# Self-attention of a perceiver block: scores in sixteen 32x32 tiles, and the residual added on TensorE

## The reference, cut to what matters

```
x = x + attn(layernorm(x))
q = (x @ w_q)  -> 16 heads of 8;   k, v = (x @ w_k), (x @ w_v) -> 4 heads of 8, each used by 4 query heads
q, k = rope(q), rope(k)
out = softmax(q k^T / sqrt(8)) v;  out = out @ w_o
```

## Time and profile before

| | |
|---|---|
| time, median of 3 runs | 803.13 us (801.89 to 804.63) |
| the profiled execution | 805.83 us, span 803.8 us |
| mean granted TensorE clock | 0.931 |
| busy: PE, DVE, ACT, POOL | 697.8, 623.8, 510.0, 395.5 us |
| self-attention pipeline | about 502 to 635 us of the span |

### The profile page before, as it was taken

The page is one execution under the profiler, slowest core; times in us unless marked ns, Lnnn a source line. Parts: engine busy times, 40 slices in busy tenths (PEclk is TensorE's granted clock), DMA queues, the critical chain, the costliest instruction groups (busy, mean ns, idle before and its releaser), DMA issues.

```text
span 803.8 us, 27728 instructions
## 1 busy us (share of the span) xinstructions
PE 697.8 (87%) x9162; PEld 563.4 (70%) x9162; DVE 623.8 (78%) x1471; ACT 510.0 (63%) x1629; POOL 395.5 (49%) x409
## 2 busy tenths in 40 slices
PE   4735999999999999999999765899999689999485
PEld 2423776777777777777777644788888578889485
DVE  6415988999999999999999668489888756759621
ACT  2633876777777777777778524688888434545152
POOL 4730664544654455455463168477777310007275
PEclk9976999999999999999999969799999759999698
DMA  7596444444444444444340030000000000006980
GB/s 164 102 208 143 84 79 86 97 86 96 86 97 85 98 85 97 84 98 83 81 84 6 3 105 1 2 3 4 0 0 3 1 1 1 1 1 197 283 264 27
DMA packets 195179, 60.76 MB, mean 76 GB/s; under 512 B 147556, under 2 KB 193512, under 8 KB 195122
## 3 DMA queue, kind: packets, MB, share of 16 engines
q1 hardware_dynamic: 192000, 55.65, 31.5%
q0 software_dynamic: 1824, 3.96, 1.4%
q10 hardware_dynamic: 1298, 0.40, 0.2%
HBM read 51.58 MB, written 8.83 MB: 75 GB/s over the span
## 4 chain that ended last, share of the span: by engine, by line
PE 49%; SPq 16%; DVE 10%; issue 9%; ACT 7%; POOL 4%; ACTq 1%; DMA 1%; DVEq 0%; POOLq 0%
PE energy L487 22%; PE bank L487 15%; PE bank L490 13%; SPq L518 8%; ACT PR L650 6%; DVE X L1778 3%; DVE STAT L1512 2%; SPq L524 2%; POOL SX L947 1%; SPq L541 1%; SPq L566 1%; POOL TQ L939 1%; SPq L577 1%; SPq L568 1%; ACTq L650 1%
## 5 line engine op out<-in xcount | busy, mean ns | idle before, releaser
L650 ACT ACTIVATE PR<-energy,STAT 128x256 f32<-128x256 f32 x512 | 234.4, 482 | 113.2 <-DVE STAT L1512 113.2
L1512 DVE TENSOR_REDUCE STAT<-energy 128x512 f32 (+1 forms) x256 | 164.2, 684 | 26.4 <-PE energy L487 26.4
L490 PE MATMUL bank<-ident,PR 128*128 128x128 f32 x1024 | 152.9, 283 | 27.8 <-DVE PT L1529 23.0
L1529 DVE COPY PT<-bank 128x512 f32<-128x512 f32 x256 | 161.8, 670 | 1.4 <-PE bank L490 1.4
L490 PEld LDWEIGHTS bank<-ident,PR 128*128 128x128 f32 x1024 | 110.1, 142 | 58.6 <-issue 46.1
L845 POOL TENSOR_TENSOR QB<-QT,headmask 128x512 f32<-128x512 f32 x32 | 33.3, 1039 | 190.4 <-DMA MK<-in_mask_BxSxS_ik 120.0
L650 ACT ACTIVATION_READ_ACCUMULATOR PR<-energy,STAT (+1 forms) x512 | 110.2, 215 | 0.0
L852 POOL TENSOR_SCALAR MZ<-MK 128x512 bf16<-128x512 int32 x64 | 94.2, 1488 | 5.3 <-DMA MK<-in_mask_BxSxS_ik 5.3
L487 PEld LDWEIGHTS bank<-wv_s,CT 128*128 128x128 f32 x512 | 67.8, 194 | 31.7 <-issue 31.7
L487 PE MATMUL bank<-PT,VT 128*32 128x128 f32 x2048 | 69.5, 276 | 0.0
L487 PE MATMUL bank<-wv_s,CT 128*128 128x128 f32 x512 | 68.5, 277 | 0.3 <-DVE OC L1521 0.2
(11 more groups left out here) (270 smaller groups left out, 1361.6 us busy)
## 6 DMA issues: line engine op xcount, KB each, us to landing
CX<-in_ctx SPq DMA_DIRECT2D x512, 32.0 KB, 2.3
MK<-in_mask_BxSxS_ik SPq DMA_DIRECT2D x128, 128.0 KB
rows_in<-fill SPq DMA_DIRECT2D x1, 3483.0 KB, 19.6
X<-in_x SPq DMA_DIRECT2D x4, 512.0 KB, 7.7
VLT<-v_last SPq DMA_DIRECT2D x4, 512.0 KB, 9.0
QT<-in_L_ffn_W SPq DMA_DIRECT2D x16, 128.0 KB
OT<-in_L_ffn_W SPq DMA_DIRECT2D x16, 128.0 KB
PAY<-rows_in SPq DMA_DIRECT2D x2, 903.0 KB, 9.2
```

The costliest lines, as they stand in the source:

```text
L490: return nc.tensor.transpose(o, i, ident[0:n, 0:n])
L650: nc.scalar.activation(PR[:, b, g, :], EB[:, g, e * KEYS:(e + 1) * KEYS], ACT.Exp, bias=STAT[:, bass.ds(t, 1), b, 1, g:g + 1].rearrange("p ...
L1512: V.tensor_reduce(STAT[:, bass.ds(t, 1), b:b + 2, 1, g:g + 1].rearrange("p a b g -> p (a b g)"), EB[:, g, :].rearrange("p (e k) -> p e k", ...
L1529: V.tensor_copy(PT[:, k % 2, e, 2 * half:2 * half + 2, :].rearrange("p g k -> p (g k)"), psum[1 if e else 7]).then_inc(ev_t, 1)
```

## The change

- Queries are ordered by group inside each 32 partitions (the weights `wqk` are laid out so), so that the 32 channels of partition block h hold one query head of each of the four key heads. The keys are now the ones spread and masked (`spread_keys`, on GpSimd, in place of spread_queries); own_keys and the clearing of KB are gone.
- scores becomes sixteen matmuls: for each sequence b and each partition block h, 32 channels x 32 queries by 128 keys, written to partitions 32b and bank h of the four energy banks. The output is the same number of scores, in another order; shift_scores and weigh_values read it so.
- The four energy banks are one buffer, and the projection has bank 1 alone: scores(t) waits for the subtraction of tile t-1, project(t) for the rotary of tile t-1.
- project_out adds ident x X[t] into the same accumulation, and ACT `evac_tokens` (in the place of own_keys) copies the sum into X; DVE's residual is gone.
- The PE list becomes await_scores(s-3), project_out(s-6), scores(s-3), project(s-1), ...: the waits of scores stay first, scores itself follows project_out.

```diff
@@ scalar
+            def evac_tokens(t, j):
+                act.wait_ge(a_wo, t + 1)
+                nc.scalar.activation(X[:, bass.ds(t, 1), :].rearrange("p a c -> p (a c)"), psum[7][:, P:2 * P],
+                                     ACT.Copy).then_inc(a_x2, 1)
+
-            def own_keys(t, j):
-
-                act.wait_ge(a_qk, t + 1)
-                wait_reuse(act, a_s, t - 3)
-                for g in range(NG):
-                    rows = slice(g * 32, g * 32 + 32)
-                    last = nc.scalar.activation(KB[rows, j, :, g, :],
-                                                QKR[rows, j, 1, :].rearrange("p (b k) -> p b k", b=BT), ACT.Copy)
-                last.then_inc(a_kb, 1)
-
-            pipeline(act, [(5, evac_probs), (2, own_keys), (0, evac_xv), (1, evac_last_values), (3, exp_scores), (5, evac_o),
+            pipeline(act, [(5, evac_probs), (6, evac_tokens), (0, evac_xv), (1, evac_last_values), (3, exp_scores), (5, evac_o),
                            (-1, centre)], NT, 4, 6)
@@ gpsimd
-            nc.gpsimd.memset(KB[:, :, :, :, :], 0.0).then_inc(zero_ok, 1)
-            def spread_queries(t, j):
+            def spread_keys(t, j):
 
                 pool.wait_ge(a_qk, t + 1)
                 nc.gpsimd.tensor_tensor(
-                    QD[:, j, :, :, :],
-                    QKR[:, j, 0, :].rearrange("p (b a q) -> p b a q", b=BT, a=1).broadcast_to([P, BT, 4, SQ]),
-                    headmask[:, :].rearrange("p (a h c) -> p a h c", a=1, c=1).broadcast_to([P, BT, 4, SQ]),
-                    ALU.mult).then_inc(a_qd, 1)
+                    KB[:, j, :, :, :],
+                    QKR[:, j, 1, :].rearrange("p (b a q) -> p b a q", b=BT, a=1).broadcast_to([P, BT, NG, SQ]),
+                    headmask[:, :].rearrange("p (a h c) -> p a h c", a=1, c=1).broadcast_to([P, BT, NG, SQ]),
+                    ALU.mult).then_inc(a_kb, 1)
@@ tensor
             def project(t, j):
                 pe.wait_ge(a_xt, t + 1)
-                wait_reuse(pe, a_tq, 2 * t - 2)
+                wait_reuse(pe, a_tq, 2 * t)
                 for w in range(4):
-                    last = mm(psum[2 + j % 2][:, w * P:(w + 1) * P], wqk[:, w, :], xt[:, j, :])
+                    last = mm(psum[1][:, w * P:(w + 1) * P], wqk[:, w, :], xt[:, j, :])
                 last.then_inc(a_p, 1)
 
+            def await_scores(t, j):
+
+                pe.wait_ge(a_qk, t + 1)
+                pe.wait_ge(a_kb, t + 1)
+                wait_reuse(pe, a_sx, t)
+
             def scores(t, j):
 
-                pe.wait_ge(a_kb, t + 1)
-                pe.wait_ge(a_qd, t + 1)
-                wait_reuse(pe, a_sx, t - 1)
                 for b in range(BT):
-                    last = mm(psum[4 + j % 2][:, b * P:(b + 1) * P],
-                              QD[:, j, b, :, :].rearrange("p h q -> p (h q)"),
-                              KB[:, j, b, :, :].rearrange("p h q -> p (h q)"))
+                    for h in range(4):
+                        rows = slice(32 * h, 32 * h + 32)
+                        last = mm(EB[32 * b:32 * b + 32, h, 0:P],
+                                  QKR[rows, j, 0, b * SQ:(b + 1) * SQ],
+                                  KB[rows, j, b, :, :].rearrange("p g k -> p (g k)"))
                 last.then_inc(a_s, 1)
 
             def project_out(t, j):
                 pe.wait_ge(a_so, t + 1)
-                mm(psum[7][:, P:2 * P], SO[:, j, :], sw_o[:, :]).then_inc(a_wo, 1)
-
-            pipeline(pe, [(3, scores), (6, project_out), (1, project), (0, turn_x), (5, weigh_values),
+                mm(psum[7][:, P:2 * P], SO[:, j, :], sw_o[:, :], stop=False)
+                mm(psum[7][:, P:2 * P], ident[:, :], X[:, bass.ds(t, 1), :].rearrange("p a c -> p (a c)"), start=False)\
+                    .then_inc(a_wo, 1)
+
+            pipeline(pe, [(3, await_scores), (6, project_out), (3, scores), (1, project), (0, turn_x), (5, weigh_values),
                           (1, self_values), (4, turn_probs)], NT, 4, 6)
@@ vector
-            def residual(t, j):
-                dve.wait_ge(a_wo, t + 1)
-                xi = X[:, bass.ds(t, 1), :].rearrange("p a c -> p (a c)")
-                V.tensor_tensor(xi, xi, psum[7][:, P:2 * P], ALU.add).then_inc(a_x2, 1)
-
-            pipeline(dve, [(4, sum_probs), (4, invert_sums), (6, residual), (3, shift_scores), (6, statistics),
+            pipeline(dve, [(4, sum_probs), (4, invert_sums), (3, shift_scores), (6, statistics),
                            (1, rotary)], NT, 4, 6)
```

More of the change, by code:

```diff
@@ L379, in perceiver_block @@
         a_kb = sem("a_kb")
-        a_qd = sem("a_qd")
         a_s = sem("a_s")
@@ L749, in evac_o @@
                 nc.scalar.activation(SO[:, j, :], psum[7][:, 0:P], ACT.Copy).then_inc(a_so, 1)
-            def own_keys(t, j):
-                act.wait_ge(a_qk, t + 1)
-                wait_reuse(act, a_s, t - 3)
-                for g in range(NG):
-                    rows = slice(g * 32, g * 32 + 32)
-                    last = nc.scalar.activation(KB[rows, j, :, g, :],
-                                                QKR[rows, j, 1, :].rearrange("p (b k) -> p b k", b=BT), ACT.Copy)
-                last.then_inc(a_kb, 1)
-            act.wait_ge(zero_ok, 1)
             act.wait_ge(n1_shift, 1)
             centre(0, 0)
-            pipeline(act, [(5, evac_probs), (2, own_keys), (0, evac_xv), (1, evac_last_values), (3, exp_scores), (5, evac_o),
+            pipeline(act, [(5, evac_probs), (6, evac_tokens), (0, evac_xv), (1, evac_last_values), (3, exp_scores), (5, evac_o),
                            (-1, centre)], NT, 4, 6)
@@ L900, in _ @@
             pool.wait_ge(ld_s, N_S)
-            pool.wait_ge(zero_ok, 2)
+            pool.wait_ge(zero_ok, 1)
             nc.gpsimd.tensor_copy(digits[:, :, :].rearrange("p r k -> p (r k)"), digit_s).then_inc(wqk_ok, 1)
-            qv = sw_q[:, :].rearrange("p (h a f) -> p h a f", h=NG * 4, a=2)
+            qv = sw_q[:, :].rearrange("p (k g a f) -> p k g a f", k=NG, g=4, a=2)
             kv = sw_k[:, :].rearrange("p (k g a f) -> p k g a f", k=NG, g=1, a=2)
@@ L906, in _ @@
                 for w, s in ((0, a), (1, 1 - a)):
-                    nc.gpsimd.tensor_copy(wqk[:, w, :].rearrange("p (h a f) -> p h a f", h=NG * 4, a=2)[:, :, a, :],
-                                          qv[:, :, s, :]).then_inc(wqk_ok, 1)
                     nc.gpsimd.tensor_copy(
-                        wqk[:, 2 + w, :].rearrange("p (k g a f) -> p k g a f", k=NG, g=4, a=2)[:, :, :, a, :],
+                        wqk[:, w, :].rearrange("p (g k a f) -> p k g a f", k=NG, g=4, a=2)[:, :, :, a, :],
+                        qv[:, :, :, s, :]).then_inc(wqk_ok, 1)
+                    nc.gpsimd.tensor_copy(
+                        wqk[:, 2 + w, :].rearrange("p (g k a f) -> p k g a f", k=NG, g=4, a=2)[:, :, :, a, :],
                         kv[:, :, :, s, :].broadcast_to([P, NG, 4, 4])).then_inc(wqk_ok, 1)
@@ L986, in normalise_probs @@
                     ALU.mult).then_inc(a_pn, 1)
-            pipeline(pool, [(2, rotate), (4, normalise_probs), (2, spread_queries)], NT, 4, 6)
+            pipeline(pool, [(2, rotate), (4, normalise_probs), (2, spread_keys)], NT, 4, 6)
             def input_rest(u, h):
@@ L1256, in weigh_values @@
                                   XV[:, (j + 1) % 4, 1, b * SQ:(b + 1) * SQ],
-                                  SP[:, j, b, g * SQ:(g + 1) * SQ])
+                                  SP[:, j, g, b * SQ:(b + 1) * SQ])
                 last.then_inc(a_o, 1)
@@ L1635, in rotary @@
                         TQ[:, j, w::2, :].rearrange("p w (b s) -> p w b s", b=BT),
-                        psum[2 + j % 2][:, :].rearrange("p (w b s) -> p w b s", w=4, b=BT)[:, w::2],
+                        psum[1][:, :].rearrange("p (w b s) -> p w b s", w=4, b=BT)[:, w::2],
                         rope[:, w, :].rearrange("p (c d s) -> p c d s", c=1, d=1)
@@ L1641, in shift_scores @@
                 dve.wait_ge(a_s, t + 1)
-                V.tensor_reduce(smx[:, j, :], psum[4 + j % 2][:, :].rearrange("p (n k) -> p n k", n=16), AX_X,
+                energy = EB[:, :, 0:P].rearrange("p h (g k) -> p h g k", g=NG)
+                V.tensor_reduce(smx[:, j, :].rearrange("p (h g) -> p h g", h=4), energy, AX_X,
                                 ALU.max).then_inc(a_mx, 1)
@@ L1645, in shift_scores @@
                 dve.wait_ge(a_mx, t + 1)
-                V.tensor_tensor(SX[:, j, :, :], psum[4 + j % 2][:, :].rearrange("p (n k) -> p n k", n=16),
-                                smx[:, j, :].rearrange("p (n a) -> p n a", a=1).broadcast_to([P, 16, SQ]),
+                V.tensor_tensor(SX[:, j, :, :].rearrange("p (h g) k -> p h g k", h=4), energy,
+                                smx[:, j, :].rearrange("p (h g a) -> p h g a", h=4, a=1).broadcast_to([P, 4, NG, SQ]),
                                 ALU.subtract).then_inc(a_sx, 1)
```

## The result

The changed kernel takes 821.3 us (median of 4 runs, 820.63 to 822.81) against 803.88 us of the kernel before, run beside it: ratio 1.0218, 95% interval 1.0186 to 1.0249. Its profiled execution has a span of 819.2 us, 15.4 more than before.

A forecast was written before the change was run, and what follows sets the result against it. A cycle of waits through project_out, evac_xv, exp and evac_o was taken to bound the changed kernel: 27 x (4.43 - 3.71) = +19.4, and 0.3, +19.7, giving 822.8 us on the timed median; range 811 to 832.

The forecast's parts named there:

- The cycle: TensorE and ScalarE: project_out waits for the previous step's evac_o; the 3.40 us loop now includes scores and becomes the bound.
- Its length: One step of the cycle: 3.40 + 0.10 + 0.22 + S = 4.43 us, between 4.13 and 4.73, against 3.71 before.
- S: Time of the sixteen small scores matmuls on TensorE, inside the cycle: 0.71 us, the middle of 0.41 and 1.01.
- Rival A: Scores on TensorE: all sixteen tiles run at once, S = 0.41, cycle 4.13 us, 814.7 us; chance 0.20.
- VectorE's relief: Residual leaves VectorE: its step falls by 0.21 us, from 3.56 to 3.35, and hides below the cycle.
- ScalarE's relief: own_keys (four copies a tile at 304 ns) goes, a 0.26 us copy comes, ahead of evac_xv's wait: worth nothing.
- GpSimd and the single buffers: Keys ready over a us before scores wants them; single energy and projection buffers freed inside 4.1 us: nothing waits.
- B: Scores on TensorE: tiles run only four at a time, S = 1.01, cycle 4.73 us, +27.8, 831 us; chance 0.15.
- C: Cycle through evac_o doesn't close because evac_o comes earlier; TensorE's own sum decides, 793 to 802 us; chance 0.11.
- D: Smaller tiles pay for the identity and the rest is hidden: within 0.3% of before; chance 0.03.
- E: TensorE idles about 0.8 us a step and loses clock: another 8 us, 831 or more; chance 0.06.
- Fill and drain: Pipeline ends: fill's shorter steps and the first project_out cancel to zero within 1 us; the last tile adds about 0.3.

The follow-up runs named there:

- e2: Kernel before with only TensorE's order changed, the waits of scores split off and scores behind project_out: 823.92 us, ratio 1.0239 to the kernel before.
- e1: Changed kernel with scores again ahead of project_out on TensorE, and a one-column matmul carrying its waits: 804.33 us, ratio 0.9997 to the kernel before.
- e3: Changed kernel with evac_o ahead of evac_xv and exp_scores in ScalarE's list: 802.45 us, ratio 0.9988 to the kernel before.
- e4: Changed kernel without identity matmul and ScalarE copy, the residual back on VectorE: 813.14 us, ratio 1.0107 to the kernel before.
- e6: Kernel before with the identity matmul and ScalarE's evac_tokens copy behind own_keys, residual out: 824.46 us, ratio 1.0276 to the kernel before.
- e7: Changed kernel with four idle 32x128 copies a tile on ScalarE, ahead of evac_tokens: 824.67 us, ratio 1.0259 to the kernel before.
- f4: Kernel of e7 with the four idle copies behind evac_tokens and ahead of evac_xv: 823.0 us, ratio 1.0239 to the kernel before.
- e8: Changed kernel with the sixteen scores matmuls reordered, partition block h outside and sequence b inside: 821.93 us, ratio 1.0225 to the kernel before.
- f1: Kernel of e3 with spread_keys ahead of normalise_probs in GpSimd's list: 800.03 us, ratio 0.9959 to the kernel before.
- e5: Kernel of e1 without identity matmul and ScalarE copy, the residual back on VectorE: 802.67 us, ratio 0.9975 to the kernel before.

## Why the prediction was right, step by step

**The cycle.** Right, and shown from four sides: its order alone makes it the bound (e2, +20 us), taking scores out shortens it to 3.59 (e1), moving evac_o ahead opens it (e3), and its length moves with what stands in it (e4, 0.22 for the identity). Forecast 822.8, range 811 to 832, measured 821.3. The signs named, TensorE waiting for ScalarE's SO and 20 us of it, are there: 19.2. The 3.40 read for it in the kernel before is in that trace as a step of its own: from project_out at 574.50 to the next is 3.41, and the next starts 0.05 after evac_o's end.

```profile
577.60 0.26 ACT L749 ACTIVATE SO<-bank 128x128 f32<-128x128 f32 x1
...
577.91 0.49 PE L487 MATMUL bank<-sw_o,SO 128*128 128x128 f32 x2
```

**Its length.** 4.43 was taken, 4.265 measured. The term that was mis-sized is S: 0.71 taken between 0.41 and 1.01, 0.43 measured. Rival A, S = 0.41, was the right one for this term. By the figure of the Trainium skill ("TensorE: Matmul & The Clock Gate", section Measured speedup vs the span model) S was an estimated 0.33; the trace has 0.43, nearer to that than to my middle.
Other terms made up for part of it. The sum said that both ends of S held the drain at a change of tiling mode; they did not hold all. project after the small tiles takes 1.00 where it took 0.89 behind 128x128 matmuls, and identity to scores is 0.31 where a matmul of its shape took 0.23: about 0.1 at each of the two changes. In e1, where project follows the 128x128 identity into the same bank, it takes 0.89 again. That agrees with the rule on mode switching of "TensorEngine Tiling (Array Packing)", section Key Properties, in the Trainium skill, which gives no price. And exp follows evac_xv by 0.28, not 0.41: 0.13 less. 4.43 - 0.28 + 0.11 + 0.06 - 0.13 = 4.19, the shorter kind of step; in the others project_out starts 0.14 and not 0.05 after evac_o. So the closeness of the forecast is in part luck: 4.265 lies a little nearer to rival A's 4.13 than to the 4.43 taken, and what lifts it above A's sum is mainly 0.11 on project and, in most steps, 0.09 on the start of project_out, which the prediction had in no term.

**VectorE's relief.** Worth nothing, as said: e4 gives it back, and the step still falls by the whole 0.22 that the prediction had put on the identity.

**ScalarE's relief.** The step that failed. "Worth nothing here", because own_keys lay in front of a wait, overlooked two things: that what stands in front of evac_xv also delays the copy of X, with weigh_values waiting for it (e6, and 0.06 in e7), and that exp starts 0.13 sooner after evac_xv in every kernel without the 32x128 copies (f4). In the changed kernel own_keys' time would cost 0.13 to 0.20 a step.

**GpSimd and the single buffers.** Hidden while the cycle bounds, as said: in the changed kernel the keys are ready 1.4 to 1.5 us before project_out starts, "over a us" as the sum had it. With the cycle open and a step of 3.7 that room is gone, and the keys are the next wait (e3).

**Rivals B, C, D, E.** B is out with S = 0.43; C and D with e2 and the waits; E with a granted clock of 1.00 in the stretch.

**Fill and drain.** Taken as 0 and +0.3; measured -2.1 and +2.6. In the fill no project_out runs and the smaller scores can show in full; from the stage's first turn_x it is 17.2 us in the changed kernel, 17.3 in e8 and 19.2 before. In the drain each tile's chain has the identity and the copy in series; without them (e4) it is 1.6 shorter, and with the order alone (e2) 1.5 longer than before. From 643 us on the clock is at 0.50, its lower level of 1.2 GHz, with TensorE busy 5.34 of 9 us; before, it was on average 0.69 in 630 to 635 us, the end of its pipeline. What that costs wasn't separated. The two errors cancel.

**The sum.** 27 x 0.551 = 14.9 with -2.1 and +2.6 is 15.4 of span, where 19.7 was forecast. That the timed medians lie 17.4 apart comes from the kernel before, whose profiled execution was 1.95 us above its median, the changed kernel's 0.3 below. Against the span the forecast is 4.3 us too high, against the medians 2.3; that 822.8 and 821.3 are only 1.5 apart owes something to the base of 803.13, where the runs beside the change gave 803.88.

## What to carry to other kernels

In a pipeline where each engine walks a fixed list, ask of every entry what it waits for and what stands behind it, and add up each cycle that comes back to the same engine one step later: moving an entry ahead or behind one wait was worth 20 us here, more than any of the work that was saved. All engines less busy and the stretch longer is the sign of such a cycle. Taking work out of it (e1) leaves it the bound if what is left is still longer than the engine's own queue, so look at what ends just before the first start of a step even where no wait is shown. And when the cycle is opened the next bound is close: here the keys, for which f1 gains 0.075 a step.

## What the runs showed of the hardware

- Sixteen fp32 matmuls of 32x32 tiles with 128 columns take 0.43 us from their start to that of the next 128x128 matmul, 0.99 for four 128x128 ones; whether four in a row share a partition block and its bank, or not, makes no difference (e8).
- Each change between 128x128 and 32x32 tiles costs about 0.1 us: project takes 1.00 behind small tiles (changed, e8) and 0.89 behind a 128x128 matmul into the same bank (e1).
- The gap from one ScalarE activation to the next, 128x256 out of PSUM and then 128x512 in SBUF, is 0.28 us in the kernels whose ScalarE makes no 32x128 copies and 0.41 in the six where it makes four a tile, whether it stood idle 0.2 or 1.25 us before. The cause stays open.
- With many small matmuls and no long waits TensorE paused 0.65 to 1.4 us at a time, three times in e1 and four times in e5, with nothing in the profile that it waited for: in written-out steps and the first trip of the loop, while 16 KB transfers of the size of the instruction queue's packets ran, and never in the later trips, in which nearly none did. The cause stays open.
